# Layer 3's cross-attention read from bytes, its second element entered in another order, layer 0's scores ahead of the contexts, and filling products around a turn

## The chip, the cores and the metric

The kernel runs on one core of one Trainium2 chip. The metric is the device time of one execution in microseconds (us). The profile tells of one execution, on that core; its engines are TensorE (PE, with its weight loads PEld), VectorE (DVE), ScalarE (ACT), GpSimd (POOL) and SyncE (SP), which issues the transfers.

## What is computed

Four layers run one after another over x (2 elements, 512 rows, 128 columns), each with the same context (2 elements, 77 rows, 128 columns).

```python
# layer 0: attention of the 10 best rows of each element over the context
scores = einsum('bnd,d->bn', x, score_w[0]) + score_b[0]
_, topk_idx = top_k(scores, 10)
x = x.at[arange(B)[:, None], topk_idx].set(attention(x[topk_idx], context))
# layer 1: one head; self-attention, cross-attention, feed-forward, a norm after each
# layer 2: 16 heads with rotary tables; norms ahead; gelu feed-forward of 512
x = x + (gelu(ln(x) @ fc1_w + fc1_b) @ fc2_w + fc2_b)
# layer 3: 16 heads, quantised to 8 bits, self-attention, then cross-attention
def _fq(x, delta, zp, n_bits):
    xq = clip(round(x / delta) + zp, 0.0, 2.0 ** n_bits - 1.0)
    return (xq - zp) * delta
sim = einsum('bhid,bhjd->bhij', _fq(q, dq, 128.0, 8), _fq(k, dk, 128.0, 8)) * SCALE
attn = softmax(sim)
out = einsum('bhij,bhjd->bhid', _fq(attn, dw, 0.0, 8), _fq(v, dv, 128.0, 8))
x = out @ wo + bo + x          # then a gated feed-forward of 2 x 512
```

The quantised attention of layer 3, _fq(attn, dw, 0.0, 8), is an integer from 0 to 255 for each of 16 x 77 keys of a row.

## The kernel before, in words

Everything stays in SBUF; the 1024 rows of x are eight tiles of 128 rows, four for each of the two elements (called 0 and 1, or halves). Every engine's program is written out by hand, one after another, with semaphores between them; there is no scheduler. Within an engine instructions run in the written order, so a wait holds back all that stands behind it on that engine.

**Layer 0.** TensorE transposes x, then three small groups (col_rows, scalars, ctx_rows, each counted in cols.turned), then the input projection in_proj (wT.turned), and then multiplies the transposed x with the score vector z3 (L0.scores). VectorE copies the columns (cols.made), the scalars, the context and z3, does some small work and then picks the ten best rows: L2050 and what follows, the top-k chain. TensorE meanwhile makes keys and values of the context for all four layers (ctx.mm), ScalarE copies them out (ctx.k, ctx.v). keep_warm are products whose result nobody reads.

**Layer 2's feed-forward.** For each half: a turn of the normalised rows (turn_half, four transposes to a bank), a copy with scale and bias by ScalarE (state_out), four hidden products of 512 columns (hidden_blocks), their activations by ScalarE, and 16 products back (out_rows). The second half's turn waits for VectorE's normalised rows.

**Layer 3's cross-attention.** For each tile i of eight, over two sets of three banks (i even, i odd):
- TensorE: scores(i); turned_maxima(i), which turns the negated maxima into rows; subtract(i), which adds them to the scores once more made; outputs(i), ten products of 128 keys each (FLAT_BLOCKS) with the values v_flat.
- VectorE: maxima(i), three reductions over the banks and three small ones that split the maximum (cross.parts); recips(i), sums and reciprocals of the exponentials; keys(i).
- ScalarE: maxima_out(i), exps(i), and rounded(i), which scales to steps of 1/255 and writes int16.
- GpSimd: the products of the exponentials with the reciprocals (flat_scaled).
- SyncE: a transposing transfer of the int16 rows (flat_rows to flat_turned), after which keys(i) limits to 255 and writes bfloat16 (flat_keys), from which outputs(i) reads.

The first element's queries are made within the self-attention before. The second element's entry is: project_half("L3.ca0", 1) on TensorE, add_to_x and moments on VectorE, rstds_of("L3.ln2", 1) on GpSimd, normal on VectorE, turn_half on TensorE, state_out on ScalarE, queries(1, 7) on TensorE, cross_queries(1, 7) on VectorE. These stand between the steps of tiles 1 to 4, since tile 4 is the second element's first. After the last tile come cross_out(1), the projection and the gated feed-forward.

In the rows, names are without numbers: q_stack and k_stack hold integers, flat_rows and flat_turned too; ps is PSUM; L650 is keep_warm; L1103, L1116 and L1124 are scores, scores once more and the maxima's products; L1109 is turned_maxima; L1132 outputs; L1980 and L1983 to L1985 are maxima; L1989 and L1990 recips; L1996 keys; L1567 rounded; L1579 exps; L597 and L498 are GpSimd's scaled product and biases.

## Time and profile before

| what | us |
|---|---|
| median of 3 runs | 516.66 (516.0 to 517.32) |
| the profiled execution | 517.13 |
| its span | 515.2 |
| PE busy | 417.2 (81%) |
| DVE busy | 354.7 (69%) |
| ACT busy | 254.5 (49%) |
| POOL busy | 238.2 (46%) |

Times in the rows count from the span's start. The profile's slices are a fortieth of the span, 12.9 us each. The shares are means over layers with different limits, so each stretch has to be read by itself. A row of the chain of work is what the end of the span can be followed back to; a row of the timeline has in brackets how long the engine idled before it, and for what.

### The profile page before, as it was taken

To read this page: it belongs to the slowest core of one execution; us is meant where nothing else is said; L and a number is where in the kernel's file an instruction comes from. 1 tells how busy PE (TensorE), PEld (TensorE's weight loads), DVE (VectorE), ACT (ScalarE), POOL (GpSimd) and SP (SyncE) were. 2 spreads that over 40 slices of the span, in tenths; PEclk is the share of its full clock that TensorE was granted. 3 is DMA by queue.
4 is the path that set the end of the run, shared out by engine and by line. 5 is a ranking of instruction groups with operands and counts; after the bars stand their busy time and mean duration, and the time that the engine had idled before them with its cause. 6 is when DMAs were issued, how large, how long until landed. Compare 5 with 4: busy or idle time off the path is not lost.

```text
span 515.2 us, 8445 instructions
## 1 busy us (share of the span) xinstructions
PE 417.2 (81%) x2920; PEld 207.4 (40%) x2920; DVE 354.7 (69%) x804; ACT 254.5 (49%) x513; POOL 238.2 (46%) x376
## 2 busy tenths in 40 slices
PE   5999878898879999988898853666685677977897
PEld 2647545543434334343336530222232222433536
DVE  1755765769997114266864389999989997689552
ACT  2224444223003766624363338899987873457441
POOL 5042234365001445416011227999998886246420
PEclk9899999999999999999999895555555555689999
DMA  9500000000000000000000004797986867113401
GB/s 257 180 1 2 3 2 0 1 0 2 1 1 1 0 2 1 1 1 1 0 2 1 1 1 52 153 152 152 148 144 126 121 122 144 27 29 73 77 0 42
DMA packets 88975, 26.10 MB, mean 51 GB/s; under 512 B 81061, under 2 KB 88167, under 8 KB 88935
## 3 DMA queue, kind: packets, MB, share of 16 engines
q1 hardware_dynamic: 88935, 25.58, 25.8%
q8 instruction: 24, 0.39, 0.3%
q14 instruction: 16, 0.13, 0.1%
HBM read 5.61 MB, written 0.52 MB: 12 GB/s over the span
## 4 chain that ended last, share of the span: by engine, by line
PE 41%; DVE 28%; POOL 20%; issue 5%; ACT 2%; DMA 2%; POOLq 0%; DVEq 0%; ACTq 0%
POOL k_stack L576 13%; DVE k_stack L2168 9%; PE ps L885 5%; PE ps L900 4%; POOL stats L567 4%; PE ps L653 3%; PE ps L760 3%; DVE stats L2257 3%; PE ps L770 2%; PE ps L650 2%; DVE xh L1731 2%; PE ps L963 2%; PE ps L861 2%; DVE st L1722 2%; PE ps L633 2%
## 5 line engine op out<-in xcount | busy, mean ns | idle before, releaser
L2257 DVE TENSOR_REDUCE stats<-ps 128x2 f32<-128x1024 f32 x64 | 77.7, 1214 | 3.1 <-PE ps L1384 2.7
L1687 ACT ACTIVATE e_buf<-ps,stats,sders 128x512 f32<-128x512 f32 x88 | 67.6, 773 | 15.8 <-POOL stats L567 15.5
L576 POOL TENSOR_SCALAR k_stack<-e_buf,stats 128x512 int16<-128x512 f32 x88 | 62.8, 725 | 2.1 <-DVE stats L2264 1.5
L1402 PE MATMUL ps<-k_stack,q_stack 128*32 128x128 bf16 x512 | 38.3, 307 | 30.8 <-DVE k_stack L2270 30.6
L1533 ACT ACTIVATE e_buf<-ps 128x1024 f32<-128x1024 f32 (+3 forms) x44 | 28.2, 711 | 54.7 <-PE ps L885 54.7
L2168 DVE TENSOR_REDUCE k_stack<-ps 128x4 f32<-128x1024 f32 (+3 forms) x32 | 45.6, 1485 | 3.2 <-PE ps L827 3.2
L1384 PE MATMUL ps<-q_stack 32*128 32x512 bf16 x128 | 37.6, 588 | 12.4 <-ACT e_buf L1687 8.9
L433 POOL TENSOR_SCALAR_AFFINE_SELECT e_buf<-e_buf 128x256 f32<-128x256 f32 x44 | 17.7, 410 | 63.5 <-ACT e_buf L1533 62.8
L1402 PEld LDWEIGHTS ps<-k_stack,q_stack 128*32 128x32 bf16 x512 | 21.9, 129 | 62.0 <-DVE k_stack L2270 59.0
L484 POOL TENSOR_SCALAR rstd<-mv 128x4 f32<-128x4 f32 x18 | 4.4, 242 | 89.5 <-DVE mv L1725 89.5
L885 PE MATMUL ps<-k_stack,q_stack 32*128 32x512 f32 (+3 forms) x256 | 34.7, 478 | 0.6 <-ACT e_buf L1533 0.4
L1687 ACT ACTIVATE t_buf<-ps,stats,sders 128x512 f32<-128x512 f32 x40 | 30.8, 774 | 7.3 <-POOL stats L567 7.3
L824 PE MATMUL ps<-q_stack,qk 32*128 32x256 f32 (+3 forms) x256 | 26.3, 477 | 8.9 <-DVE k_stack L2168 8.0
L1866 DVE COPY v_rows<-ps 128x512 f32<-128x512 f32 x16 | 11.0, 688 | 29.8 <-PE ps L900 22.9
L567 POOL TENSOR_SCALAR stats<-stats,sders 128x2 f32<-128x2 f32 x64 | 23.4, 365 | 16.0 <-DVE stats L2257 15.7
L1454 ACT ACTIVATE xT<-ps,cols 128x512 f32<-128x512 f32 x16 | 12.4, 777 | 35.1 <-PE ps L633 35.1
L1767 DVE TENSOR_TENSOR x<-ps,x 128x512 f32<-128x512 f32 x14 | 9.6, 689 | 27.8 <-PE ps L760 15.2
L2270 DVE TENSOR_SCALAR k_stack<-k_stack 128x1024 bf16<-128x1024 int16 x64 | 27.5, 434 | 1.8 <-DMA k_stack<-k_stack 1.8
L576 POOL TENSOR_SCALAR k_stack<-t_buf,stats 128x512 int16<-128x512 f32 x40 | 28.3, 717 | 0.5 <-DVE stats L2264 0.2
L1731 DVE TENSOR_SCALAR xh<-x,mv,rstd 128x128 f32<-128x128 f32 x68 | 19.3, 347 | 11.6 <-POOL rstd L486 11.5
L760 PE MATMUL ps<-l_w,e_buf 128*128 128x128 f32 x192 | 22.6, 277 | 2.4 <-ACT e_buf L1514 2.4
L760 PEld LDWEIGHTS ps<-l_w,e_buf 128*128 128x128 f32 x192 | 21.9, 192 | 5.5 <-ACT e_buf L1514 3.4
(288 smaller groups left out, 899.0 us busy)
## 6 DMA issues: line engine op xcount, KB each, us to landing
wsq<-in_squares SPq DMA_DIRECT2D x3, 384.0 KB, 5.0
k_stack<-k_stack SPq DMA_TRANSPOSE x64, 3.1
...
```

The source lines that it names most:

```text
L567: pool.tensor_scalar(stats[:, 1, c:c + 2], stats[:, 0, c:c + 2], sders[:, 8:9], None, ALU.mult).then_inc(S("ints.m"), 1)
L576: pool.tensor_scalar(t_rows[n % TURNING][:, j, :], e_ring[n % len(e_ring)][:, j, :], stats[:, 2, c:c + 1], 0.0, ALU.mult, ALU.add).then_in ...
L760: mm = pe.matmul(o, tile(hid[:, c, :], k * QB + t), w2[:, c, :], start=(c == 0), stop=(c == FC - 1))
L885: mm = pe.matmul(ps[:, 2 * slot + j % 2, 0:N - kb * P], k1[r, v, b * N + kb * P:b * N + (kb + 1) * P], q_shift[r, b, v, kb * P:N], start=T ...
L1384: mm = pe.matmul(ps[:, 2 * (n % 3) + j % 2, :], tile(q_int, b * QB + qb)[r, :], k_band[r, v, b * N:(b + 1) * N], start=True, stop=True)
L1402: mm = pe.matmul(ps[BAND * band:BAND * (band + 1), 7 - b, qb * P:(qb + 1) * P], v_band[:, kb, b, V * band + v, :], t_keys[n % len(t_keys)] ...
L1533: act.activation(e_ring[n % len(e_ring)][:, :, 0:N - kb * P], ps[:, 2 * (n % 3):2 * (n % 3) + 2, 0:N - kb * P], ACT.Exp).then_inc(S("heads ...
L1687: act.activation(e_ring[n % len(e_ring)][:, j, :], ps[:, 2 * (n % 3) + j, :], ACT.Exp, bias=stats[:, 1, c:c + 1], scale=sders[:, 8:9], acc ...
L1731: ins = dve.tensor_scalar(xh[:, t, :], x[:, t, :], mv[:, t, 0:1], rstd[:, t:t + 1], ALU.subtract, ALU.mult)
L2168: dve.tensor_reduce(nm, ps[:, FILL_BANK[n]:FILL_BANK[n] + 4, c:c + (qb + 1) * P], AX, ALU.max, negate=True).then_inc(S("heads.max"), 1)
L2257: dve.tensor_reduce(stats[:, 0, c:c + 2], ps[:, 2 * (n % 3):2 * (n % 3) + 2, :], AX, ALU.max, negate=True).then_inc(S("ints.nm"), 1)
L2270: dve.tensor_scalar(t_keys[n % len(t_keys)], t_turned[n % TURNING], QMAX, None, ALU.min).then_inc(S("ints.pt"), 1)
```

## The change

1. **Bytes.** GpSimd fills both flat_rows once with the words 0x64006400. rounded(i) writes unsigned bytes to the low byte of each 16-bit word, so each word read as float16 is 1024 plus the integer. The transfer turns them as before; keys(i) goes, and outputs(i) reads flat_turned as float16 with one product more, the values vc3 times a constant of -1024. vc3 and v_flat become float16. The buffers of flat_keys are added to flat_turned, six in all, and the transfer waits for cross.pv instead of cross.keys.
2. **The second element's entry.** TensorE projects ahead of subtract(1), makes scores(2) ahead of it too, and turns and projects the queries within tile 3; filling products fall from 11 and 4 to 5 and 2. VectorE does largest(2) (the three large reductions) ahead of normal, and cross_queries ahead of recips(2). ScalarE does rounded(0) ahead of exps(1). GpSimd adds its two biases at tiles 1 and 2 instead of tile 5.
3. **Layer 0.** The scores stand ahead of the context's and in_proj's transposes; z3 is copied straight from PSUM after the first group. The contexts are made in the order 1, 2, 0, and 3 later in place of filling products; the swapped keys of layer 2 are made later too.
4. **Products around a turn.** Three filling products ahead of the turn of L2.ln3's second half, and three behind it.

```diff
+CTX_BANK, CTX_ORDER = (0, 6, 7, 2), (1, 2, 0, 3)
...
+BYTE_BASE = 1024.0
+TWO_HIGH = float(np.array([0x64006400], np.uint32).view(np.float32)[0])
...
-        vc3 = sb("vc3", [M, B, D], BF16)
+        vc3 = sb("vc3", [M, B, D], F16)
...
+        flat_turned += [a.bitcast(I16) for a in flat_keys]
+        flat_keys = [a.bitcast(F16) for a in flat_turned]
+        minus_base = sb("minus_base", [M, P], F16)
+
+        def low_bytes(a):
+            return a.bitcast(U8).rearrange("p (n two) -> p n two", two=2)[:, :, 0]
...
-                        sp.wait_ge(S("cross.keys"), i - len(flat_turned) + 1)
+                        sp.wait_ge(S("cross.pv"), i - len(flat_turned) + 1)
+                    if i == 3:
+                        sp.wait_ge(S("ints.pv"), PAIRS)
...
                     if i == 1:
+                        add_bias("L3.co", "L3.ln2.xh", 0, 1)
                         rstds_of("L3.ln2", 1)
-                    if i == 5:
-                        for h in range(B):
-                            add_bias("L3.co", "L3.ln2.xh", h, B)
+                    if i == 2:
+                        pool.wait_ge(S("cross.q"), B)
+                        add_bias("L3.co", "L3.ln2.xh", 1, B)
...
+                    for rows in flat_rows:
+                        pool.memset(rows.bitcast(F32), TWO_HIGH).then_inc(S("L3.flat.high"), 1)
+                    pool.memset(minus_base[:, :], -BYTE_BASE).then_inc(S("L3.minus"), 1)
...
-                    pe.wait_ge(S("cross.keys"), i + 1)
+                    pe.wait_ge(*turned(PAIRS + i))
+                    pe.wait_ge(S("L3.minus"), 1)
+                    pe.matmul(ps[:, 6 + b, t * P:(t + 1) * P], vc3[:, b, :], minus_base[:, :], start=True, stop=False)
                     for c in range(FLAT_BLOCKS):
                         mm = pe.matmul(ps[:, 6 + b, t * P:(t + 1) * P], v_flat[:, b, c, :],
-                                       tile(flat_keys[i % len(flat_keys)], c), start=(c == 0),
+                                       tile(flat_keys[i % len(flat_keys)], c), start=False,
...
                     for i in range(2, T + FLAT_VALUES_BEHIND):
+                        if i == QB - 1:
+                            turn_half(xh, "L3.ln2.xh", 1, bank=7)
                         if i == QB:
-                            queries(1, 7)
                             subtract(i - 1)
-                            keep_warm(6, 4, half(q_int, 0))
+                            keep_warm(6, 2, half(q_int, 0))
                             pe.wait_ge(S("cross.q"), B)
                         if i < T:
                             scores(i)
-                        if 2 < i <= T and i != QB:
+                        if i == QB - 1:
+                            turned_maxima(2)
+                            queries(1, 7)
+                        if i <= T and i != QB:
                             subtract(i - 1)
                         if i == 2:
-                            keep_warm(6, 11, half(q_int, 0))
-                        if i == QB - 1:
-                            turn_half(xh, "L3.ln2.xh", 1, bank=7)
+                            keep_warm(6, 5, half(q_int, 0))
...
-                        if i < T:
+                        if 2 < i < T:
                             turned_maxima(i)
...
-            pe.transpose(ps[:, 2, 0:NCOL], col_rows[:, :], ident[0:NCOL, 0:NCOL]).then_inc(S("cols.turned"), 1)
+            pe.transpose(ps[:, 5, 0:NCOL], col_rows[:, :], ident[0:NCOL, 0:NCOL]).then_inc(S("cols.turned"), 1)
             pe.wait_ge(S("scalars.loaded"), 16)
             pe.matmul(ps[:, 2, 64:73], ones_row[:, :], scalar_row[:, :], start=True, stop=True
                       ).then_inc(S("cols.turned"), 1)
+            pe.wait_ge(S("L0.z3"), 1)
+            pe.wait_ge(S("L0.xT"), B)
+            for b in range(B):
+                mm = pe.matmul(ps[0:2, 4, :], z3[:, 1 - b:3 - b], half(xT, b), start=(b == 0), stop=(b == 1))
+            mm.then_inc(S("L0.scores"), 1)
...
-            for layer, (wk, wv, bv) in enumerate(ctx_w):
-                bank = (5, 6, 7, 0)[layer]
+
+            def context(layer):
+                wk, wv, bv = ctx_w[layer]
+                bank = CTX_BANK[layer]
...
-            pe.wait_ge(S("ctx.k"), 3)
-            pe.matmul(ps[:, 1, 0:B * M], swap[:, :], kc[:, 2, :], start=True, stop=True).then_inc(S("ctx.swapped"), 1)
-
-
+            for layer in CTX_ORDER[:3]:
+                context(layer)
             pe.wait_ge(S("L0.flags.sb"), 1)
-            pe.wait_ge(S("ctx.v"), 1)
             for b in range(B):
...
-            keep_warm(3, 2, zeros)
+            pe.wait_ge(S("ctx.k"), 3)
+            pe.matmul(ps[:, 1, 0:B * M], swap[:, :], kc[:, 2, :], start=True, stop=True).then_inc(S("ctx.swapped"), 1)
...
-            pe.wait_ge(S("ctx.k"), 4)
-            pe.wait_ge(S("ctx.v"), 4)
+            pe.wait_ge(S("ctx.v"), 3)
...
-            keep_warm(2, 10, zeros)
+            context(CTX_ORDER[3])
+            keep_warm(3, 5, zeros)
...
+                spare_columns = q_stack[:, 6 * NT:6 * NT + N]
+                pe.wait_ge(S("L3.v.base"), 1)
                 pe.wait_ge(S("heads.e"), count("L2.ca", "e") + 2 * B * V)
                 hidden_blocks("L2.ff", l2_w1, HIDDEN_2, range(2))
                 last_turn()
                 hidden_blocks("L2.ff", l2_w1, HIDDEN_2, range(2, FC))
                 second_outputs()
                 out_rows("L2.ff", l2_w2, 0, OUTPUTS_2)
+                keep_warm(5, 3, spare_columns)
                 turn_half(xh, "L2.ln3.xh", 1, bank=7)
+                keep_warm(5, 3, spare_columns)
                 hidden_blocks("L2.ff", l2_w1, HIDDEN_2, range(FC, B * FC))
                 out_rows("L2.ff", l2_w2, 1, OUTPUTS_2)
...
-                subtract(1)
...
-                    act.activation(flat_rows[i % len(flat_rows)][:, 0:FLAT], flat_e[i % len(flat_e)], ACT.Identity,
+                    act.wait_ge(S("L3.flat.high"), len(flat_rows))
+                    act.activation(low_bytes(flat_rows[i % len(flat_rows)][:, 0:FLAT]), flat_e[i % len(flat_e)], ACT.Identity,
...
+                rounded(0)
                 exps(1)
-                rounded(0)
+                state_out("L3.ca", col("L3_xattn_ln2_g"), col("L3_xattn_ln2_b"), [1], 7)
                 maxima_out(2)
                 for i in range(3, T + FLAT_ROUND_BEHIND):
                     if i <= T:
                         exps(i - 1)
-                    if i == QB - 1:
-                        state_out("L3.ca", col("L3_xattn_ln2_g"), col("L3_xattn_ln2_b"), [1], 7)
...
-            for layer, bias in enumerate((col("L0_xattn_in_proj_b", 1), None, col("L2_xattn_ca_bk"), None)):
-                act.wait_ge(S("ctx.mm"), layer + 1)
-                bank = (5, 6, 7, 0)[layer]
+
+            def context_out(turn):
+                layer = CTX_ORDER[turn]
+                bias = (col("L0_xattn_in_proj_b", 1), None, col("L2_xattn_ca_bk"), None)[layer]
+                act.wait_ge(S("ctx.mm"), turn + 1)
+                bank = CTX_BANK[layer]
...
+            for turn in range(3):
+                context_out(turn)
...
+            context_out(3)
...
-                def keys(i):
-                    dve.wait_ge(*turned(PAIRS + i))
-                    if i >= len(flat_keys):
-                        dve.wait_ge(S("cross.pv"), i - len(flat_keys) + 1)
-                    dve.tensor_scalar(flat_keys[i % len(flat_keys)], flat_turned[i % len(flat_turned)], QMAX, None,
-                                      ALU.min).then_inc(S("cross.keys"), 1)
-
                 def rest():
-                    for i in range(2, T + FLAT_KEYS_BEHIND):
+                    for i in range(2, T + FLAT_SUMS_BEHIND):
                         if i == 2:
                             add_to_x("L3.ca0", 6, [1])
                             moments("L3.ln2", 1, "L3.ca0.x", 1)
+                            largest(2)
+                            normal("L3.ln2", 1)
+                            parts(2)
+                        if i == QB:
+                            cross_queries(1, 7)
                         if 2 < i < T + FLAT_SUMS_BEHIND:
                             recips(i - FLAT_SUMS_BEHIND)
-                        if i == QB:
-                            cross_queries(1, 7)
-                        if i < T:
+                        if 2 < i < T:
                             maxima(i)
-                        if i == 2:
-                            normal("L3.ln2", 1)
                         if i == T + 1:
                             add_to_x("L3.co", 6, [0])
                             stats_of("L3.co.x", 0, range(QB))
                             means_of(0)
-                        if i >= FLAT_KEYS_BEHIND:
-                            keys(i - FLAT_KEYS_BEHIND)
                     normal("L3.ln3", 0)
 
                 return maxima, recips, rest
             ins.then_inc(S("bands.made"), 1)
             dve.memset(z3[:, :], 0.0)
             then(dve.memset(l0_zero, 0.0))
...
+            dve.wait_ge(S("cols.turned"), 1)
+            dve.tensor_copy(z3[:, 1:2], ps[:, 5, COL["L0_xattn_score_w"]:COL["L0_xattn_score_w"] + 1]).then_inc(S("L0.z3"), 1)
             dve.wait_ge(S("cols.turned"), 3)
-            dve.tensor_copy(cols[:, :], ps[:, 2, 0:NCOL]).then_inc(S("cols.made"), 1)
+            dve.tensor_copy(cols[:, :], ps[:, 5, 0:NCOL]).then_inc(S("cols.made"), 1)
             then(dve.tensor_copy(scalars[:, :], ps[:, 2, 64:73]))
             dve.tensor_copy(ctxT[:, :], ps[:, 2, 128:128 + B * M]).then_inc(S("ctxT.made"), 1)
             dve.wait_ge(S("cols.made"), 1)
-            dve.tensor_copy(z3[:, 1:2], col("L0_xattn_score_w")).then_inc(S("L0.z3"), 1)
```

On TensorE in layer 0, from the columns' transpose on (ident turns rows; z is the score vector; wsq and wT are weights, ctxT the context), before:

```order
L1195 MATMUL ps<-ident,col_rows 128x39
L1197 MATMUL ps<-scalar_row,ones_row 128x9
L1201 MATMUL ps<-ident,ctx_rows 128x77 x2
L1205 MATMUL ps<-ident,in_proj 128x128 x4
L1211 MATMUL ps<-xT,z 2x512 x2
L1222 MATMUL ps<-ctxT,wT 128x154
```

and now:

```order
L1217 MATMUL ps<-ident,col_rows 128x39
L1219 MATMUL ps<-scalar_row,ones_row 128x9
L1224 MATMUL ps<-xT,z 2x512 x2
L1228 MATMUL ps<-ident,ctx_rows 128x77 x2
L1232 MATMUL ps<-ident,in_proj 128x128 x4
L1246 MATMUL ps<-ctxT,wsq 128x154
```

The scores (xT,z) moved ahead of two groups, and the first context is one that needs no wT.

On TensorE at the second element's entry, from the last outputs of the self-attention on (wsq,xT x4 is the projection, xT,wsq the query product, ident,xh the turn), before:

```order
L1402 MATMUL ps<-k_stack,q_stack 32x128 x8
L1116 MATMUL ps<-km,q_stack 128x308
L1124 MATMUL ps<-kc,max_turned 128x462 x2
L1124 MATMUL ps<-kc,max_turned 128x308
L797 MATMUL ps<-wsq,xT 128x128 x4
L1103 MATMUL ps<-km,q_stack 128x462 x2
L1103 MATMUL ps<-km,q_stack 128x308
L650 MATMUL ps<-q_stack,ident 128x512 x11
L1109 MATMUL ps<-ident,max_parts 32x128
```

and now:

```order
L1429 MATMUL ps<-k_stack,q_stack 32x128 x8
L815 MATMUL ps<-wsq,xT 128x128 x4
L1121 MATMUL ps<-km,q_stack 128x462 x2
L1121 MATMUL ps<-km,q_stack 128x308
L1134 MATMUL ps<-km,q_stack 128x308
L1142 MATMUL ps<-kc,max_turned 128x462 x2
L1142 MATMUL ps<-kc,max_turned 128x308
L668 MATMUL ps<-q_stack,ident 128x512 x5
L651 MATMUL ps<-ident,xh 128x128 x4
L1121 MATMUL ps<-km,q_stack 128x462 x2
```

subtract(1) moved behind the projection and scores(2), and the turn ahead of scores(3).

On VectorE around tile 4 (ta and q_stack<-ta are the second element's queries), before:

```order
L1989 TENSOR_REDUCE cr_sum<-e_buf 128x16
L1990 RECIPROCAL cr_rec<-cr_sum 128x16
L1848 TENSOR_SCALAR ta<-ps,sders 128x512
L1849 TENSOR_SCALAR ta<-ta 128x512
L1854 TENSOR_SCALAR q_stack<-ta 128x512
L1980 TENSOR_REDUCE cr_pair<-ps 128x6 x2
L1980 TENSOR_REDUCE cr_pair<-ps 128x4
L1983 TENSOR_REDUCE max_parts<-cr_pair 128x16
L1984 TENSOR_REDUCE cr_pair<-max_parts 128x16
L1985 TENSOR_REDUCE max_parts<-cr_pair 128x16
L1996 TENSOR_SCALAR k_stack<-q_stack 128x1280
```

and now:

```order
L1880 TENSOR_SCALAR ta<-ps,sders 128x512
L1881 TENSOR_SCALAR ta<-ta 128x512
L1886 TENSOR_SCALAR q_stack<-ta 128x512
L2027 TENSOR_REDUCE cr_sum<-e_buf 128x16
L2028 RECIPROCAL cr_rec<-cr_sum 128x16
L2009 TENSOR_REDUCE cr_pair<-ps 128x6 x2
L2009 TENSOR_REDUCE cr_pair<-ps 128x4
L2017 TENSOR_REDUCE max_parts<-cr_pair 128x16
L2018 TENSOR_REDUCE cr_pair<-max_parts 128x16
L2019 TENSOR_REDUCE max_parts<-cr_pair 128x16
```

The queries moved ahead of recips(2), and the keys at the end are gone, here and in seven further places.

## Rows read from the trace of the kernel before

**Rows 1.** The page: the chain's shares, and the granted clock in 40 slices (tenths).
```profile
PE 41%; DVE 28%; POOL 20%; issue 5%; ACT 2%; DMA 2%; POOLq 0%; DVEq 0%; ACTq 0%
...
PEclk9899999999999999999999895555555555689999
```

**Rows 2.** Timeline: start us, us, engine, line, operation, count, idle before and its cause.
```profile
283.19 0.66 PE L633 MATMUL ps<-ident,xh 128*128 128x128 f32 x4 [0.85 <-DVE xh L1731]
284.72 5.40 PE L770 MATMUL ps<-xT,l_w 128*128 128x512 f32 x8 [0.87 <-ACT xT L1454]
...
39.61 0.81 PE L650 MATMUL ps<-k_stack,ident 128*128 128x512 bf16 x3
```

**Rows 3.** Windows: busy us of PE, PEld, DVE, ACT, POOL; clock, DMA share, GB/s.
```profile
285.50:286.00 0.50, 0.50 (x2) 0.24 (x1) 0.00 (x0) 0.00 (x0) 0.50 (x1) 0.59 0.00 0
453.00:453.50 0.50, 0.50 (x2) 0.27 (x2) 0.50 (x1) 0.50 (x2) 0.00 (x0) 0.50 0.00 0
```

**Rows 4.** The chain of work in order of time, layer 1: start us, us, what.
```profile
77.07 3.45 PE ps L770 x8
```

**Rows 5.** Timeline of layer 0, TensorE and VectorE.
```profile
8.03 0.52 PE L1201 MATMUL ps<-ident,ctx_rows 77*128 77x77 f32 x2
8.66 0.20 DVE L2034 COPY cols<-ps 128x39 f32<-128x39 f32 x1 [3.96 <-PE ps L1201]
9.40 3.41 PE L1211 MATMUL ps<-xT,z 128*2 128x512 f32 x4
12.93 0.74 DVE L2050 TENSOR_SCALAR e_buf<-ps,scalars 2x512 f32<-2x512 f32 x1 [3.17 <-PE ps L1211]
```

**Rows 6.** The chain of work, layer 0.
```profile
17.09 0.46 PE ps L1222 x2
17.55 0.44 PE ps L1225 x4
...
25.81 2.40 PE ps L650 x10
```

**Rows 7.** Timeline of ScalarE and TensorE at the second element's entry.
```profile
440.37 0.69 ACT L1608 ACTIVATE xT<-ps,sders 128x512 f32<-128x512 f32 x1 [0.38 <-PE ps L1402]
...
441.77 2.08 PE L797 MATMUL ps<-wsq,xT 128*128 128x128 f32 x8
...
452.73 0.23 PE L1109 MATMUL ps<-ident,max_parts 128*32 128x128 bf16 x1 [2.10 <-DVE max_parts L1985]
```

**Rows 8.** The chain of work in layer 3's cross-attention.
```profile
447.97 1.03 DVE xh L1731 x4
449.00 1.35 DVE cr_sum L1989
...
450.63 1.43 DVE cr_pair L1980 x3
...
460.40 0.40 DVE k_stack L1996
...
464.48 0.63 DVE k_stack L1996
...
469.06 2.70 POOL x L498 x2
```

**Rows 9.** Timeline of VectorE, the second element's queries.
```profile
455.59 0.75 DVE L1848 TENSOR_SCALAR ta<-ps,sders 128x512 f32<-128x512 f32 x1 [1.28 <-PE ps L653]
```

**Rows 10.** Timeline of ScalarE, rounded; and ScalarE's strided output, by its line.
```profile
474.00 1.32 ACT L1567 ACTIVATE q_stack<-e_buf,sders 128x1232 int16<-128x1232 f32 x1 [0.33 <-POOL e_buf L597]
...
L1664 ACT ACTIVATE v_one<-ps x2: 597/598/599, 99.7 to 111.7; 128x512 f32<-128x512 f32 x2
```

**Rows 11.** The chain of work, from the last transfer to the gated feed-forward.
```profile
482.27 3.35 DMA q_stack<-q_stack
...
486.05 1.12 DVE xh L1731 x4
...
488.86 1.07 PE ps L784 x2
```

23 lines of the change are left out of this document (12 added, 11 removed).

## Prediction

> **What bounds the kernel now.** I read the chain of the page and its clock row first [rows 1]. No engine bounds the whole span: TensorE leads the chain (41%), VectorE has 28%, GpSimd 20%, and the granted clock stands at half from the 24th slice to the 34th. So the change is worth what the stretches are worth that it touches. There are three: layer 0 (5 to 32 us), the feed-forward of layer 2 (278 to 295 us), and layer 3's cross-attention (433 to 489 us), where the chain runs for the most part over VectorE. Layers 1 and 2's attention and the self-attention of layer 3 keep their instructions; they only move in time.
>
> **Layer 2, products around a turn.** At 282.35 TensorE has finished the first half's outputs, waits 0.85 us for the normalised rows, turns them in 0.66 us, and waits 0.87 us for the scaled state [rows 2]. Then the granted clock falls, 0.59 over the half microsecond from 285.5 [rows 3], the lower of the levels 2.4 and 1.2 GHz from there. The four hidden products (8 records) take 5.40 us [rows 2]; the same eight in layer 1 took 3.45 on the chain [rows 4]. The stretch is on the chain, since the last activation and then the second outputs follow its last product. Three added products at 0.27 us each (L650 in [rows 2]) end near 283.1, before the rows are there at 283.15, and three behind the turn end near 284.6, before the state is there at 284.7. Both threes lie in idle time and cost nothing; were the rows earlier by 0.8 us, they would cost up to 0.8. Idle time on either side falls from about 0.86 to 0.1 us. If the clock stays up, the gain is 5.40 - 3.45 = **1.95**; the other end is 0. I take 1.95, since what stood before the fall was just this idle time. Beside it a rule of the Trainium skill (TensorE: Matmul & The Clock Gate, Part 1: The HAM clock gate): the hardware's look at the activity is free-running and not tied to the kernel, so that the place of a change of clock varies. By that rule the dip could come elsewhere instead of vanishing; it is rival 2.
> GpSimd gets three memsets (two of 128x640 words, one of 77x128) after the one of v_band. It idles some 20 us there and TensorE's new wait for that memset is long fulfilled by 272 us: 0.
>
> **Layer 0.** The score products take 3.41 us from 9.40, behind four small groups [rows 5]. They now stand ahead of the context and in_proj transposes. The vector z is copied after the columns' transpose, near 7.85, and the second state copy ends at 7.96, so they start at 8.10, when TensorE is free, and end at 11.51. But VectorE's next instructions now wait for three column groups, and the third (ctx_rows, 0.45 us net [rows 5]) stands behind the scores: the copy L2034 starts at 12.07 instead of 8.66, and from it to the first top-k instruction L2050 VectorE has 1.03 us of small work (8.66 to 9.75 less the moved copy), which before was hidden by the scores. L2050 starts at 13.1 against 12.93 [rows 5]: +0.2, not -1.3. Queued behind this wait on VectorE is the whole top-k chain, and ScalarE's copies of the contexts wait for cols.made.
> The contexts then come in the order 1, 2, 0 and end near 17.9, before the flags are broadcast; the fourth (0.46 + 0.44 = 0.90 us [rows 6]) goes where ten filling products stood, of which five stay. The ten took 2.40 us and ended at 28.21 [rows 6], some 0.5 us after the probabilities were there. Now it is 26.0 + 0.9 + 1.2 = 28.1. Layer 0 gives **-0.1**. Bounds: the half clock of 23 to 26 us vanishes (-1.2), or it lasts over the contexts too (+2).
>
> **Layer 3, the entry of the second element.** Before, TensorE begins the projection at 441.77 though its input was there at 440.37 + 0.69 = 441.06 [rows 7]: subtract(1) stood ahead. It now begins at 441.1 and takes the same 2.08 (half clock). VectorE's sum, statistics and mean then end at 445.2. After that largest(2), 1.46, ends at 446.65; GpSimd, with one bias more (1.35, half of L498 x2 in [rows 8]) between its first product and the rstd, ends at 446.7; the four normal instructions 1.03 [rows 8] -> 447.8; the parts 0.6 -> 448.4. The turn on TensorE (0.66) and the state (0.78) come to 449.4, the query product (0.86 at full clock) to 450.5. Scores(2) now comes before subtract(1), so exps(1) starts at 445.65 instead of 441.88 and ends at 447.2; its reader, recips(1), starts at 448.4 only, so the 3.8 us are covered by 1.2. VectorE goes on without a gap: recips(1) 1.63 (449.00 to 450.63 [rows 8]) -> 450.05, maxima(3) 2.06 -> 452.1, the queries 1.79 [rows 9] -> 453.9, recips(2) -> 455.55, maxima(4) -> 457.65. GpSimd's second bias waits for those queries, runs to 455.3, and scaled(2) queued behind it waits for recips(2) at 455.55 anyway: 0. Before, maxima(4) ended at 460.40 [rows 8], since VectorE had idled 1.28 us for a query product [rows 9] on a clock that stood at 0.50 [rows 3] behind an idle time of 2.10 us [rows 7] and 0.82 for scores(4). Gain **2.75**. Below that, if the clock is at half here too, turn, scores, queries and subtract cost about 2 more; above, nothing further.
>
> **Layer 3, no keys.** Eight instructions L1996 go; in the cycles 4 to 6 they are 0.40 + 0.63 + 0.63 [rows 8]: VectorE is without a gap there, a cycle is 4.08 to 4.32 (460.40 to 464.48 the first), and becomes 3.68: **-1.66**. What is late next? ScalarE has 1.59 + 0.27 + 1.32 (L1567 [rows 10]) = 3.2 us in a cycle, GpSimd 2.25, TensorE 3.3 with its fillings; and the loop over a pair of banks (maxima 2.06, turned maxima and copy 0.5, subtract 0.9, exps 1.6, scores 1.2) is 6.3 for two cycles. VectorE stays last. Then from parts(7) to the end of recips(7): the two biases (2.70 [rows 8]) no longer stand ahead of scaled(5). Now recips(6) or, longer, copy, rounded(5) 1.32, exps(7) 1.59 and recips(7) 1.63 give 5.05 against 5.47: **-0.4**. The tail: the last transpose lands 3.35 us after it is issued [rows 11]; then stood keys 0.40, normal 1.12, turn 0.66, projection 0.99. The rows are now normalised and ready, behind it stand outputs(7) 0.65 + 0.06 for the added product, ScalarE's copy 0.7 and the projection: from recips(7) to the first feed-forward product 9.6 instead of 10.3: **-0.7**. The eight added products (K = 77, 128 columns, some 0.06 each like their neighbours L1132) lie in filled time but for the last. TensorE now waits for the transpose itself and five behind; for tiles 0 to 3 that has landed long before. Transposes now may run six deep, without a wait for pv that matters.
> Unknown is the byte write: ScalarE writes 1232 bytes with a step of two where it wrote 1232 int16 in 1.32 us [rows 10]. No row has a byte output. Lower end 1.3, since its reads stay; upper end four times that, 5.3. I take 1.32, since this engine's strided writes of f32 (L1664, groups of 8 of 9 words) take 0.60 for 512 [rows 10], 1.17 ns each against 1.07 ns in the 1.32 for 1232.
>
> **The sum.** 0.1 + 1.95 + 2.75 + 1.66 + 0.4 + 0.7 = 7.56. The profiled execution took 517.13 (span 515.2 and 1.9 around it), so 509.6. The median of the three is 516.66, 0.5 below the profiled one; I keep 509.6 for both, as 0.5 is less than the unknowns.
>
> **Rivals.**
> 1. Forecast: all terms as above, 508.4 to 510.6. Chance 0.52.
> 2. A half-clock stretch stays: in layer 2 in spite of the fillings, or in the entry of layer 3. It is for it that TensorE's filling there falls from 11 + 4 to 5 + 2 products, against it that the idle time of 2.10 us goes. Each costs about 1.95 (5.40 against 3.45): 511.5, both 513.5. Chance 0.22.
> 3. The freed VectorE finds another engine late: if the bank loop or exps(1) is 1 us longer than I have it, the cycles and the biases' term (2.1) stay at their old length: 511.7. For it speaks that scores(2) and subtract(1) are later than before, against it that 1.2 us are left. Chance 0.14.
> 4. Layer 0's dip goes too, or the L3 fillings that shrink were in the way: 508 or less. Chance 0.08.
> 5. Slower: the byte write. With r us for one, ScalarE's cycle is 1.9 + r + 0.1; over r = 1.7 it bounds, and five cycles (r - 1.7) and the last one (r - 1.32) use up the 7.56 at r = 2.9. At 5.3 it would be 18 + 4 - 7.6 above 517.13: 531. Chance 0.04.
>
> **How the numbers follow.** The likeliest is 1, so 509.6. Range 507.6 to 512.9: case 4 is in down to 0.4 below its 508, above the forecast case 3 and one dip; out are two dips and case 5. A measurement of this kernel tells 0.3% (1.55 us) from no change, that is 515.1. Only case 5 and a pile-up of 2 and 3 come near: faster 0.94, same 0.03, slower 0.03.
>
> **What would show it.** In the changed profile: granted clock 1.00 from 283 to 295 and L770's second eight at 3.45; L2050's successor at 13.1, not 11.7; the first copy of max_turned for tile 4 near 457.7 less the shift of what lies before (2.0); cycles of 3.7 there; the byte activation at 1.3; from the landing of the last transpose to the first gated product 2.5 us. A byte activation over 1.7, a clock under 1.00 in the entry, or gaps on VectorE between parts(4) and recips(7) would make it wrong.

## The result, and the profile after

The changed kernel takes 519.79 us (median of 8 runs, 518.38 to 523.5) where the kernel before takes 517.41 (8 runs, 516.0 to 519.76): the ratio is 1.0054, with a 95% interval of 1.0033 to 1.0076. It is slower: by 2.4 us between the medians, by 2.8 us by the ratio, and the ratios are used where parts are added up below. I had forecast 509.6, and faster. The profiled execution of the changed kernel took 519.41, with a span of 517.6 beside the 515.2 of before.

I read the clock row of the page first, since [rows 1] shows its counterpart of before. The changed kernel's page, chain by engine and granted clock in 40 slices of 12.9 us:

```profile
PE 41%; DVE 28%; POOL 19%; issue 5%; ACT 4%; DMA 2%; POOLq 0%; DVEq 0%; ACTq 0%
...
PEclk9699999999999999999689996555555555689999
```

The shares of the chain have hardly moved. The clock row has: the second slice stands at 6 where it was 8, and there is a new 6 and 8 in the 20th and 21st slice, near 250 us, where nothing was forecast; the 8 of the 23rd slice, at the turn of layer 2, is gone. The windows of these two stretches in the changed kernel, and of the second one before (columns: window, length, busy us with counts of PE, PEld, DVE, ACT and POOL, granted clock, DMA share, GB/s):

```profile
18.00:29.00 11.00, 10.67 (x52) 8.18 (x53) 4.87 (x13) 1.59 (x6) 0.00 (x0) 0.53 0.13 41
...
251.00:262.00 11.00, 11.00 (x52) 3.32 (x46) 5.50 (x10) 2.04 (x2) 0.00 (x0) 0.50 0.00 0
```

```profile
251.00:262.00 11.00, 9.45 (x80) 5.46 (x76) 9.13 (x17) 2.34 (x3) 0.00 (x0) 1.00 0.01 1
```

Between 251 and 262 us TensorE is busy all the time and gets through 52 records, where before, at the full clock, it got through 80.

To place the loss I take the same instructions in both chains of work (start us, us, what). They are the first projection of layer 1, the first hidden product of layer 2, the activation behind its second eight, and the first cross maxima and the first gated product of layer 3. The kernel before:

```profile
34.32 1.95 PE ps L653 x4
...
272.34 1.72 PE ps L770 x4
...
290.15 0.70 ACT e_buf L1514
...
432.85 1.49 DVE cr_pair L1980 x3
```

The changed kernel:

```profile
36.91 1.95 PE ps L671 x4
...
281.27 1.72 PE ps L788 x4
...
293.64 3.71 PE ps L788 x8
297.38 0.70 ACT e_buf L1540
...
440.36 1.49 DVE cr_pair L2009 x3
...
491.79 0.86 PE ps L802 x2
```

| stretch | lateness at its end, us | change in it | forecast |
|---|---|---|---|
| layer 0, to the projection | 36.91 - 34.32 = +2.59 | +2.59 | -0.1 |
| to the hidden products of layer 2 | 281.27 - 272.34 = +8.93 | +6.34 | 0 |
| the turn in layer 2 | 297.38 - 290.15 = +7.23 | -1.70 | -1.95 |
| self-attention of layer 3 | 440.36 - 432.85 = +7.51 | +0.28 | 0 |
| cross-attention of layer 3 | 491.79 - 488.86 [rows 11] = +2.93 | -4.58 | -5.5 |
| from there to the end of the span | 517.6 - 515.2 = +2.4 | -0.5 | 0 |

So the gains came, at 6.3 of the 7.5 us, and two losses that the sum did not hold took 8.9. The larger stands in a stretch of layer 2 in which I had counted three memsets of GpSimd at nothing. The timeline of GpSimd there, in the changed kernel (start us, us, engine, line, operation, shapes, count, idle time before):

```profile
240.52 3.51 POOL L621 MEMSET q_stack<- 128x4096 bf16 x1
243.97 1.20 POOL L623 MEMSET q_stack<- 128x640 f32 x2
245.11 0.20 POOL L624 MEMSET minus_base<- 77x128 f16 x1
245.28 2.23 POOL L627 TENSOR_TENSOR kc<-ident 32x1232 bf16<-32x1232 f32 x1
```

The engine does idle long (25 us here, 20 before), but behind the product of L627, which makes over_keys. The memsets stand ahead of it and push it 1.4 us later. VectorE and TensorE in the same stretch of the changed kernel:

```profile
245.83 2.24 DVE L1874 SCALAR_TENSOR_TENSOR ta<-qk,cos_t 128x512 f32<-128x512 f32 x1 [0.34 <-PE ps L888]
```

```profile
249.45 0.66 PE L879 MATMUL ps<-ident,v_rows 128*128 128x128 f32 x4 [1.66 <-DVE qk L1876]
```

The same instructions in the kernel before: GpSimd's product and its next instruction, 20 us later, and the VectorE instruction, which runs twice:

```profile
241.41 2.23 POOL L609 TENSOR_TENSOR kc<-ident 32x1232 bf16<-32x1232 f32 x1
263.70 0.23 POOL L484 TENSOR_SCALAR rstd<-mv 128x4 f32<-128x4 f32 x1 [20.06 <-DVE mv L1725]
```

```profile
217.59 0.69 DVE L1842 SCALAR_TENSOR_TENSOR ta<-qk,cos_t 128x512 f32<-128x512 f32 x1 [4.34 <-PE ps L870]
...
243.25 0.95 DVE L1842 SCALAR_TENSOR_TENSOR ta<-qk,cos_t 128x512 f32<-128x512 f32 x1 [0.34 <-PE ps L870]
```

```profile
245.58 0.66 PE L861 MATMUL ps<-ident,v_rows 128*128 128x128 f32 x4 [0.36 <-DVE qk L1844]
```

L1874 multiplies the raw queries by the scale and by a cosine table: two operands of 128x512 read from SBUF. It ends at 248.07, 0.56 us behind the end of GpSimd's product at 247.51, as if it had stood still until then. TensorE is idle for 1.66 us instead of 0.36, and then its clock falls: it is at half from 250.1 to 263.9 us, and TensorE is busy throughout.

In layer 0 the timeline of TensorE shows two idle times behind the score products that before were none:

```profile
12.92 0.53 PE L1246 MATMUL ps<-ctxT,wsq 128*128 128x154 f32 x2 [0.69 <-ACT wT L1470]
...
17.91 0.92 PE L1258 MATMUL ps<-t_buf,ident 2*128 2x512 bf16 x2 [0.64 <-ACT t_buf L1470]
```

**Theory A**: both losses are idle time of TensorE that brings its lower clock. In layer 2 it comes from the memsets, by way of the overlap of GpSimd's product with a VectorE instruction. **Rival B**: the half clock near 250 us comes with the shift of 2.6 us out of layer 0, or in a rhythm of its own, and the overlap is beside it. **Rival C**: in layer 0 it is the kind of product (few columns) and not the idle time.

The price of the layer 2 loss can be split in the profiled executions: the products of L879 start at 249.45 instead of 245.58, which is 3.87 later, 2.59 of it from layer 0 and so 1.3 of it new. The other 5.1 of the 6.34 come behind them.

### The profile page after: what moved, and what is told of

Its sections match the earlier page's. It is cut to its first block, busy times and chain, and to the rows that moved or that the text cites. A ratio compares the mean times of both kernels' runs of the same rounds, so it can differ in the third digit from the quotient of the medians.

```text
span 517.6 us, 8429 instructions
## 1 busy us (share of the span) xinstructions
PE 418.3 (81%) x2907; PEld 209.7 (41%) x2919; DVE 352.1 (68%) x796; ACT 254.4 (49%) x513; POOL 239.8 (46%) x379
## 4 chain that ended last, share of the span: by engine, by line
PE 41%; DVE 28%; POOL 19%; issue 5%; ACT 4%; DMA 2%; POOLq 0%; DVEq 0%; ACTq 0%
POOL k_stack L590 13%; DVE k_stack L2199 9%; PE ps L903 5%; PE ps L918 4%; POOL stats L581 4%; PE ps L778 3%; PE ps L671 3%; DVE stats L2288 3%; PE ps L668 2%; PE ps L788 2%; PE ps L879 2%; PE ps L981 2%; DVE xh L1763 2%; DVE st L1754 2%; PE ps L651 2%
## 5 line engine op out<-in xcount | busy, mean ns | idle before, releaser
L590 POOL TENSOR_SCALAR k_stack<-t_buf,stats 128x512 int16<-128x512 f32 x40 | 28.4, 720 | 0.5 <-DVE stats L2295 0.2
L778 PEld LDWEIGHTS ps<-l_w,e_buf 128*128 128x128 f32 x192 | 21.9, 192 | 5.5 <-ACT e_buf L1540 3.4
```

What stands on the lines that cost most here:

```text
L590: pool.tensor_scalar(t_rows[n % TURNING][:, j, :], e_ring[n % len(e_ring)][:, j, :], stats[:, 2, c:c + 1], 0.0, ALU.mult, ALU.add).then_in ...
L778: mm = pe.matmul(o, tile(hid[:, c, :], k * QB + t), w2[:, c, :], start=(c == 0), stop=(c == FC - 1))
```

## The experiments

Each was timed in turn with the kernel before on the same chip. There were three such groups, e1 to e4, e5 to e8 and e9 to e12, each on a chip of its own, and the median of the kernel before was 517.1 to 517.4 in them. A difference between two kernels of different groups is therefore best taken from the ratios; where I give it from the medians I add the other.

| kernel | median us | ratio to before, 95% |
|---|---|---|
| e1_memsets_later | 513.54 | 0.9945 (0.9925 to 0.9964) |
| e2_old_layer0 | 509.76 | 0.9864 (0.9840 to 0.9888) |
| e3_before_memsets | 523.00 | 1.0126 (1.0102 to 1.0151) |
| e4_before_layer0 | 520.24 | 1.0074 (1.0050 to 1.0098) |
| e5_no_fillings | 512.13 | 0.9889 (0.9854 to 0.9924) |
| e6_old_entry | 513.96 | 0.9930 (0.9904 to 0.9956) |
| e7_fill_wait | 515.18 | 0.9958 (0.9934 to 0.9981) |
| e8_layer0_filled | 511.05 | 0.9873 (0.9847 to 0.9900) |
| e9_fillings_alone | 514.96 | 0.9953 (0.9930 to 0.9975) |
| e10_bytes_alone | 515.24 | 0.9970 (0.9942 to 0.9997) |
| e11_entry_alone | 514.00 | 0.9933 (0.9906 to 0.9961) |
| e12_product_first | 509.42 | 0.9844 (0.9809 to 0.9879) |

**e1_memsets_later.** The three memsets go behind the first bias of the feed-forward of layer 2.

```diff
                     pool.memset(v_band[:, :, :, :, :], 0.0).then_inc(S("L3.v.base"), 1)
-                    for rows in flat_rows:
-                        pool.memset(rows.bitcast(F32), TWO_HIGH).then_inc(S("L3.flat.high"), 1)
-                    pool.memset(minus_base[:, :], -BYTE_BASE).then_inc(S("L3.minus"), 1)
                     hi, rest = (ident[0:2 * H, k * H:(k + 1) * H].unsqueeze(2).broadcast_to([2 * H, H, M])
...
                     add_bias("L2.ff", "L2.ln3.xh", h, h + 1)
+                    if stop >= 3 and h == 0:
+                        for rows in flat_rows:
+                            pool.memset(rows.bitcast(F32), TWO_HIGH).then_inc(S("L3.flat.high"), 1)
+                        pool.memset(minus_base[:, :], -BYTE_BASE).then_inc(S("L3.minus"), 1)
```

> The changed kernel with GpSimd's three added memsets moved behind the bias of L2.ff of the first element, some 20 us later. In the changed kernel they stand ahead of the product that makes over_keys (2.23 us), which then runs from 245.28 to 247.51, over VectorE's L1874, which takes 2.24 us instead of 0.95; TensorE waits 3.6 us for it instead of 2.3 and its granted clock is at half from 250 to 263. Theory A (that overlap is the cause): the product ends near 246.2, L1874 takes about 1.0, the clock stays up, and the kernel takes 519.8 - 6.3 = 513.5. Rival B (the fall of the clock comes with the shift of everything by 2.6 us that layer 0 causes, whatever GpSimd does): half a dozen us of half clock stay, 518.5 to 519.8.

It took 513.54. The same memsets with the same contents, in another place, are worth 6.2 us (5.6 by the ratios), and the half clock near 250 us is gone although the shift of layer 0 is still there. VectorE's instruction, TensorE's products behind it, and the window:

```profile
246.93 0.96 DVE L1875 SCALAR_TENSOR_TENSOR ta<-qk,cos_t 128x512 f32<-128x512 f32 x1 [0.34 <-PE ps L889]
```

```profile
249.27 0.66 PE L880 MATMUL ps<-ident,v_rows 128*128 128x128 f32 x4 [0.37 <-DVE qk L1877]
```

```profile
251.00:262.00 11.00, 9.41 (x74) 4.26 (x71) 8.57 (x17) 2.64 (x3) 0.00 (x0) 1.00 0.00 0
```

Rival B falls by this for the kernel with both.

**e3_before_memsets.** The other side of it: the kernel before, with the memsets ahead of the product and nothing else.

```diff
                     pool.memset(v_band[:, :, :, :, :], 0.0).then_inc(S("L3.v.base"), 1)
+                    for rows in flat_rows:
+                        pool.memset(rows.bitcast(F32), TWO_HIGH).then_inc(S("L3.flat.high"), 1)
+                    pool.memset(minus_base[:, :], -BYTE_BASE).then_inc(S("L3.minus"), 1)
```

> The kernel before with nothing but GpSimd's three memsets added ahead of the product of over_keys (their contents are not used). Theory A: that product then starts at 242.8 instead of 241.4 and ends at 245.0, VectorE's L1842 that starts at 243.25 takes 2.3 instead of 0.95, and the half clock follows: 517.4 + 6.3 = 523.7; if only the delay comes and no half clock, 518.8. Rival B (no overlap cost; the clock follows the shift of layer 0): 517.4.

It took 523.00, slower by 1.26%, which is 6.5 us. Its timelines of GpSimd, VectorE and TensorE, and a window:

```profile
242.98 2.23 POOL L616 TENSOR_TENSOR kc<-ident 32x1232 bf16<-32x1232 f32 x1
```

```profile
243.53 2.24 DVE L1849 SCALAR_TENSOR_TENSOR ta<-qk,cos_t 128x512 f32<-128x512 f32 x1 [0.33 <-PE ps L877]
```

```profile
247.15 0.66 PE L868 MATMUL ps<-ident,v_rows 128*128 128x128 f32 x4 [1.65 <-DVE qk L1851]
```

```profile
250.00:262.00 12.00, 12.00 (x58) 3.95 (x52) 6.05 (x13) 2.04 (x2) 0.00 (x0) 0.50 0.00 0
```

The product ends at 245.21 and L1849 at 245.77, again 0.56 later; TensorE idles 1.65 us and is at half from 248.3 to 262.0. Layer 0 is the old one here, so no shift is needed for it, and rival B falls altogether. Three memsets of 1.4 us together, on an engine with nothing urgent to do, cost six and a half.

**e7_fill_wait.** This splits the loss into the delay and the clock. The changed kernel as it is, with filling products in the idle time.

```diff
                     outputs(1)
+                    pe.wait_ge(S("L3.v.base"), 1)
+                    after("e", 4)
+                    keep_warm(4, 5, q_stack[:, 6 * NT:6 * NT + N])
                     pe.wait_ge(S("L2.ca.q"), B)
```

> The changed kernel as it is, memsets ahead of over_keys, with five filling products (0.27 us each) where TensorE waits 1.66 us for VectorE's L1874, ahead of the turn of the first heads. Theory A (the overlap costs 1.3 us of delay, and the idle time it leaves on TensorE brings the half clock, which costs 5): the clock stays up near 250 us and the kernel takes 519.8 - 5.0 = 514.8. Rival B (the clock falls there for another reason): 519.8.

It took 515.18, against 519.79 without the fillings and 513.54 without the overlap. In its trace VectorE's instruction still takes 2.25 us, TensorE's idle time is 0.48 and the clock stays up:

```profile
248.82 1.25 PE L668 MATMUL ps<-q_stack,ident 128*128 128x512 bf16 x5
250.55 0.66 PE L879 MATMUL ps<-ident,v_rows 128*128 128x128 f32 x4 [0.48 <-DVE qk L1879]
```

```profile
251.00:262.00 11.00, 9.61 (x74) 3.78 (x72) 8.99 (x19) 2.56 (x3) 0.00 (x0) 1.00 0.00 0
```

So of the loss 4.6 us is the half clock behind the idle time (519.79 - 515.18; 5.0 by the ratios, give or take 1.7), and what is left is the delay: 1.6 by the medians (515.18 - 513.54), only 0.7 by the ratios, give or take 1.6. The trace tells it better than the times: the lengthened instruction is 2.24 - 0.95 = 1.29. What keeps the clock up is the five products in the wait; whether it is that TensorE is less idle or that these products are of another kind, this run does not separate.

**e12_product_first.** GpSimd's product goes ahead of the memset of v_band, which then is what runs beside VectorE's instruction. The edit, on e2_old_layer0 (below):

```diff
-                    pool.memset(v_band[:, :, :, :, :], 0.0).then_inc(S("L3.v.base"), 1)
...
                     pool.tensor_tensor(over_keys, hi, rest, ALU.add).then_inc(S("L3.over"), 1)
+                    pool.memset(v_band[:, :, :, :, :], 0.0).then_inc(S("L3.v.base"), 1)
```

> e2_old_layer0 with GpSimd's product for over_keys ahead of the memset of v_band (3.5 us) instead of behind it. The product then runs from 238.9 to 241.1, while VectorE has nothing to do, and it is the memset that runs beside VectorE's L1866. Theory A (only an instruction of GpSimd that reads two operands holds VectorE up, a memset does not): L1866 takes 0.69 instead of 0.96, 509.8 - 0.3 = 509.5. Rival B (any instruction of GpSimd does): L1866 waits for the end of the memset and takes 1.0 or more, 509.8 to 510.3.

It took 509.42, against 509.76: as forecast, but the times alone can't tell 0.3 us. The trace can. GpSimd's two instructions and VectorE's:

```profile
237.50 2.23 POOL L621 TENSOR_TENSOR kc<-ident 32x1232 bf16<-32x1232 f32 x1
239.69 3.50 POOL L622 MEMSET q_stack<- 128x4096 bf16 x1
```

```profile
242.79 0.69 DVE L1866 SCALAR_TENSOR_TENSOR ta<-qk,cos_t 128x512 f32<-128x512 f32 x1 [0.34 <-PE ps L887]
```

The memset runs until 243.19, 0.4 us into L1866, and L1866 takes 0.69, which is also what the same instruction takes at 217.59 in the kernel before; it is held by the product and not by the memset. The kernel before already paid 0.26 us here (0.95 at 243.25).

**e4_before_layer0** and **e2_old_layer0.** Layer 0 by itself: in the first it is the only change to the kernel before, in the second it is the one part left out of e1_memsets_later. The core of the edit (+ as in the changed kernel):

```diff
+            for b in range(B):
+                mm = pe.matmul(ps[0:2, 4, :], z3[:, 1 - b:3 - b], half(xT, b), start=(b == 0), stop=(b == 1))
+            mm.then_inc(S("L0.scores"), 1)
             pe.wait_ge(S("ctx.loaded"), 16)
...
-            for layer, (wk, wv, bv) in enumerate(ctx_w):
+            for layer in CTX_ORDER[:3]:
+                context(layer)
...
-            keep_warm(2, 10, zeros)
+            context(CTX_ORDER[3])
+            keep_warm(3, 5, zeros)
```

> The kernel before with only layer 0 changed. Theory A: TensorE is idle for 0.7 and 0.6 us behind the score products, its clock is at half from 18 to 29 us instead of 23 to 26, and the first projection of layer 1 starts 2.6 us later; nothing else changes: 520.0. Rival B (the shift also brings the half clock near 250 us): 525 or so. Rival C (the long half clock in layer 0 was one execution's): 517.3.

> The changed kernel with the memsets moved as in e1_memsets_later and layer 0 in the order of the kernel before. Theory A: the first projection of layer 1 is back at 34.3 us instead of 36.9, so 2.6 less than e1_memsets_later: 510.9, which is the sum that was predicted without the errors of layer 0 and of the memsets. Rival B: with the shift gone the half clock at 250 us is gone too, whether or not the memsets are moved, so also about 511; e3_before_memsets tells the two apart. Rival C (gains of layer 3 and the fillings are lost elsewhere when the rest moves): over 513.

e4 took 520.24, slower by 0.74%, or 3.8 us (2.6 to 5.1); the spans of the two profiled executions differ by 2.8. Its half clock in layer 0 lasts from 17.7 to 28.1 us, the projection of layer 1 starts at 36.87, and near 250 us it has no half clock: the shift alone does not bring it. Rival C of its expectation, that one execution alone had it, falls too. e2 took 509.76, a median of four runs. That is near the forecast of 509.6, reached by leaving out the two things that the forecast priced at about nothing, and in part by luck, as the terms missed on both sides (below). What I expected of e2 was 510.9: against e1 the old layer 0 is worth 3.8 us and not 2.6. The two traces differ by 1.8 us at the projection of layer 1 and by 4.1 at the end, and the one of e1 has stretches at half, at 67 to 71 and 456 to 460 us, that the one of e2 has not. One window of e4:

```profile
18.00:28.00 10.00, 9.66 (x45) 7.28 (x45) 3.98 (x12) 1.27 (x4) 0.00 (x0) 0.50 0.16 51
```

**e8_layer0_filled.** Fillings in the two idle times of the new layer 0, on e1_memsets_later.

```diff
+            pe.wait_ge(S("heads.base"), 1)
+            keep_warm(1, 2, k_stack[:, 8 * NT:8 * NT + N])
             pe.wait_ge(S("wT.made"), 1)
...
                 context(layer)
+            keep_warm(1, 2, k_stack[:, 8 * NT:8 * NT + N])
             pe.wait_ge(S("L0.flags.sb"), 1)
```

> e1_memsets_later (new layer 0, 513.5) with two filling products in each of the two idle times of TensorE in layer 0 (0.69 us ahead of the contexts, 0.64 us ahead of the flags). Theory A (these idle times bring the long half clock from 19 us): it comes at 22 us or later as in the kernel before, and the kernel takes 510.0, within 1 us. Rival B (the half clock comes with the kind of products there, few columns or two rows, idle or not): 513.5.

It took 511.05, 2.5 less than without the four fillings (3.7 by the ratios). TensorE's timeline, and two windows:

```profile
12.77 0.53 PE L1249 MATMUL ps<-ctxT,wsq 128*128 128x154 f32 x2 [0.26 <-ACT wT L1474]
...
17.05 0.61 PE L669 MATMUL ps<-k_stack,ident 128*128 128x512 bf16 x2
17.76 0.60 PE L1262 MATMUL ps<-t_buf,ident 2*128 2x512 bf16 x2
```

```profile
18.00:21.00 3.00, 2.84 (x21) 1.88 (x19) 2.36 (x8) 0.50 (x2) 0.00 (x0) 1.00 0.43 137
22.00:24.00 2.00, 2.00 (x10) 1.15 (x10) 0.71 (x3) 0.19 (x1) 0.00 (x0) 0.50 0.03 8
```

By the granted clock it now falls at 21.3 instead of 19.5 and is back at 24.8 instead of 29.8; the projection starts at 34.37, as before. Rival C keeps a part: with the one idle time at 0.26 and the other gone there is still a fall near 21 us, as in most kernels with the old layer 0. The early start and the length go away with the fillings. But a filling takes idle time away and at the same time puts a product of 512 columns among those of few, so this run does not tell theory A from rival C; no run does. (In this execution a second stretch at half, 35.0 to 38.5 us, took 1.7 us back.) The new order of layer 0 gains nothing even then.

**e9_fillings_alone, e10_bytes_alone, e11_entry_alone, e5_no_fillings, e6_old_entry.** The three parts that were to gain, each alone on the kernel before (e10 with its memsets in the later place), and e2_old_layer0 without the fillings or without the entry. The edit of e9, which e5 takes back:

```diff
+                keep_warm(5, 3, spare_columns)
                 turn_half(xh, "L2.ln3.xh", 1, bank=7)
+                keep_warm(5, 3, spare_columns)
```

Of e11, which e6 takes back, the core on VectorE:

```diff
                             moments("L3.ln2", 1, "L3.ca0.x", 1)
+                            largest(2)
+                            normal("L3.ln2", 1)
+                            parts(2)
+                        if i == QB:
+                            cross_queries(1, 7)
                         if 2 < i < T + FLAT_SUMS_BEHIND:
                             recips(i - FLAT_SUMS_BEHIND)
-                        if i == QB:
-                            cross_queries(1, 7)
```

Of e10, on VectorE and ScalarE:

```diff
-                        if i >= FLAT_KEYS_BEHIND:
-                            keys(i - FLAT_KEYS_BEHIND)
...
-                    act.activation(flat_rows[i % len(flat_rows)][:, 0:FLAT], flat_e[i % len(flat_e)], ACT.Identity,
+                    act.activation(low_bytes(flat_rows[i % len(flat_rows)][:, 0:FLAT]), flat_e[i % len(flat_e)], ACT.Identity,
```

> The kernel before with only the two threes of filling products around the turn of layer 2. In the kernel before the clock fell at 285.5 and the second eight hidden products took 5.4 us; in e5_no_fillings, with neither fillings nor that fall, they took 3.7. Theory A (the fillings keep the clock up where it would fall): 517.2 - 1.7 = 515.5. Rival B (whether the clock falls there hangs on more than this idle time, and the fall comes somewhere else): 517.2, with a stretch at half at another place.

> The kernel before with only the byte part (no keys on VectorE, memsets behind the first bias of L2.ff). By the prediction's terms 1.66 for the cycles and 0.7 for the tail: 517.2 - 2.4 = 514.8. The byte activation takes 1.3 us, like the int16 one. Rival (what VectorE gets free is lost to the wait for the query product in the entry): 516.

> The kernel before with only the second element's entry reordered in layer 3, and the biases of GpSimd. By the prediction's terms 2.75 for the entry and 0.4 for the biases: 517.2 - 3.1 = 514.1; by e6_old_entry, which lost 4.2 against e2_old_layer0, as low as 513.0. Rival (a half clock in the entry takes the 2 us back): 516.

> e2_old_layer0 without the two threes of filling products around the turn of layer 2. If they are what keeps the clock up there, the second eight hidden products take 5.4 us again instead of 3.7: 509.8 + 1.7 = 511.5. Rival (the clock would have stayed up in any case in this kernel, as it did in e3_before_memsets): 509.8.

> e2_old_layer0 with the second element's entry of layer 3 in the order of before (bytes, fillings and later memsets stay). The prediction priced that entry at 2.75: 512.5. The trace of e2_old_layer0 from the first cross maxima to the first gated product is 5.3 us shorter than before, 0.2 short of the sum of the parts for layer 3. Rival (the byte part alone brings most of it, since what it frees on VectorE is where the entry waits): 510.5 or less.

By the ratios, and 517.2 for before, the three gains and their intervals are these: the fillings alone gave 2.4 us (1.3 to 3.6), the bytes 1.6 (0.2 to 3.0) and the entry 3.5 (2.0 to 4.9). The forecasts were 1.95, 2.4 and 3.1. Together they give 7.5; e2_old_layer0, which holds all three, gained 7.0. With e4's +3.8 and e3's +6.5 the sum of all five is +2.8, and the changed kernel is slower by 2.8 (1.0054). The parts add up, within the some 3 us that their intervals leave together.

Three of these runs had rivals. e9's, that the fall would only come elsewhere, is not borne out: its trace has no stretch at half between 25.8 and 305 us. e10's was 516, for the case that what VectorE gets free is lost in the entry; the interval (514.2 to 517.0) holds that as well as the 514.8 of the forecast, so e10 does not decide. e11's was 516 for a half clock in the entry, and its interval (512.3 to 515.2) leaves it out. e6, which gives up the new entry and keeps the rest, took 513.96: that is 3.4 us more than e2 by the ratios (4.2 by the medians), where the terms of the prediction give 3.15 and the rival in its expectation 0.7 or less. In the traces the stretch from the first cross maxima to the end of recips(7) is 44.66 us in e6 and 40.81 in e2. So the entry is worth its price beside the bytes too.

e5 was 512.13 where I had 511.5 or 509.8, but its trace does not show what I had expected. Its second eight hidden products run at the full clock without the fillings. It is 0.25 us behind e2 at the first cross maxima and 2.06 behind at those of tile 4, and what is lost there is lost to a half clock from 447.3 to 450.8, in layer 3's entry:

```profile
285.65 3.70 PE L787 MATMUL ps<-xT,l_w 128*128 128x512 f32 x8 [0.87 <-ACT xT L1474]
```

```profile
285.00:290.00 5.00, 3.70 (x8) 1.44 (x8) 2.07 (x11) 3.27 (x5) 2.94 (x4) 1.00 0.00 0
448.00:450.00 2.00, 2.00 (x8) 0.73 (x8) 1.86 (x3) 1.05 (x2) 0.55 (x1) 0.50 0.00 0
```

With the fillings the clock stayed up at this turn in all eight profiled kernels that have them; without them it fell in four (before, e4, e10, e11) and not in two (e3, e5). So the idle time makes the fall likely, and does not settle it. Nor does e5 show what the fillings are worth: e8 and e12, which have them, have a stretch at half in the entry too. Their worth rests on e9.

## Why the prediction was wrong

**What bounds.** The reading of the stretches was right. Wrong were two terms put at about zero, the memsets at 0 and layer 0 at -0.1, and both by the same omission: I priced what a step waits for on its own engine and did not carry the new idle time of TensorE into the clock. That the clock is what the idle time costs is shown for the memsets (e7); for layer 0 it is the likeliest reading (e8).

**The memsets: the step that failed.** The prediction says that GpSimd "idles some 20 us there" and writes 0. It asked for TensorE's wait on the memset, which was long fulfilled, but not what stands behind the memsets on GpSimd's own queue. That is a product of 2.23 us, and 1.4 us later it lies over an instruction of VectorE that TensorE waits for. The price was 6.34 in the profiled executions: 1.3 of delay, the rest half clock (e7). The warning was in the trace of before: there L1842 takes 0.95 us at 243.25 where it takes 0.69 at 217.59, and it ends at 244.20, again 0.56 behind the end of the product (243.64). The Trainium skill (SBUF — State Buffer, Who interferes with whom) has the rule: a VectorE instruction with two SBUF inputs contends with a GpSimd instruction that reads SBUF, not with one that only writes. The traces agree on both halves: 2.24 us beside the product, 0.69 beside the memset. I had not weighed it.

**Layer 0: -0.1 forecast, +2.59 measured, and 2 was the upper bound.** The single instructions came as worked out: the scores ended at 11.51, and the top-k chain began at 12.90 (forecast 13.1). But TensorE then waited 0.69 for the copy of wT, which I had not listed as queued behind the scores. And its contexts ended at 17.27, not 17.9, so 0.64 of idle time stood ahead of the flags, where before the fourth context had been. I moved that context to where ten fillings stood and counted it as a fair exchange; it had been a filling itself. The clock fell at 18.0 us and returned at 28.4, instead of 22.7 and 26.2.

**Layer 2's turn: right in kind, 0.25 too much.** The eight products took 3.71 at the full clock, not 3.45 as in layer 1; the gain was 5.41 - 3.71 = 1.70. That it was the fillings is shown less firmly than the time: see e5 and e9.

**The entry: right, where the clock was.** In e2_old_layer0 the first cross maxima start at 431.67, 1.18 earlier than before. With that added back, the projection starts at 441.13 (forecast 441.1), recips(1) ends at 450.06 (450.05), maxima(3) at 452.11 (452.1) and maxima(4) at 457.49 (457.65). The gain at that point is 2.91 (2.75). The prediction names a clock under 1.00 in the entry as a sign against it. There was one, 437.0 to 443.9 in e2, over the projection, which the sum had priced at half; it cost nothing that was not in the sum. In the changed kernel there was a second one, from 461.8 to 465.3, on scores(4) and the seven fillings behind it. Its chain:

```profile
462.38 1.03 PE ps L1121 x3
463.40 2.47 PE ps L668 x7
465.87 0.16 PE ps L1127
```

Counted from the first cross maxima, VectorE starts recips(4) 0.83 later here than in e2. Most of that it has lost ahead of the fillings: it waited 0.69 for scores(4), which took 1.23 us instead of 0.69, and began maxima(4) 0.73 later. The seven fillings (1.67 in e2) are on the chain, but add only 0.10. That is the 0.75 by which the cross-attention gained less here (4.58) than in e2 (5.33), and all that is left of rival 2 in layer 3.

**The bytes: right.** A byte activation takes 1.31 to 1.33 us, and rival 5 never came near. The cycles of VectorE in the changed kernel are 3.75, 3.92 and 3.68 from maxima to maxima; 3.68 was forecast, and the longest holds a wait of 0.15 for exps. From maxima(4) to parts(7) e2 gained 1.5 (forecast 1.66); from there to the end of recips(7) 0.46 (0.4). The tail gained 0.44, not 0.7: from the landing to the gated product it took 2.77 and not 2.5. The cross-attention as a whole was 5.33 shorter in e2 against 5.5.

**The rivals.** Rival 2 was the right worry in the wrong place. It named a rule of the Trainium skill (TensorE: Matmul & The Clock Gate, Part 1: The HAM clock gate), that the place of a change of clock varies. The traces agree: in kernels with the same old layer 0 the fall came at 21.9, 22.3, 22.7 or 24.0 us, and in e3 and e6 not at all (e3 has one at 64.0 instead, in layer 1). But I let it take back only gains that I had listed. A new half clock in a stretch that the change touches through a third engine had no rival and no chance, and the 3% for slower was put on the byte write.

The kernel with the lowest median is e12_product_first, with the bytes, the entry and the fillings, the old layer 0, GpSimd's product first and the memsets last: 509.42 us, 1.6% (1.2 to 1.9) below the kernel before; the times do not tell it from e2_old_layer0.

What stays open: why the clock did not fall at the turn of layer 2 in e3 and e5, whose instructions there are those of before; whether it is the idle time or the kind of product that brings the long half clock in layer 0; and 0.3 of the 0.5 us that the changed kernel gained behind the start of the gated feed-forward (0.2 is its first product, 0.86 instead of 1.07). Single executions differ by where the clock falls, and so a term of 2 us that rests on it can't be read from one trace.
